# Two-layer transformer kernel, last layer: routing scores spread over scratch memory, scaled rows one batch later, the last network's chunks one at a time inside the last batch's chain

## The chip, the core and the metric

One core of a Trainium2 chip. TensorE (matrix products), VectorE, ScalarE, GpSimd and SyncE work in parallel, each through its own instructions in order; they wait for one another by semaphores. The metric is the device time of one execution, in microseconds.

## The reference

Input x is 8 batches x 256 tokens x 128. Six steps follow, each added to x: self-attention with 16 heads of 8; cross-attention with one head; an expert network; causal attention with one head; cross-attention with 16 heads; and the last network, which matters here:

```python
light_out = feedforward(x, gamma_l, w1_l, b1_l, w2_l, b2_l)
s = jnp.einsum('bnd,d->bn', x, routing_token)
scores = coor_descent(s, N_ITERS, effective_k, EPS)      # 50 steps
selected_scores, selected_indices = jax.lax.top_k(scores, NUM_HEAVY)
routed = jnp.take_along_axis(x, selected_indices[..., None], axis=1)
routed_out = feedforward(routed, gamma_h, w1_h, b1_h, w2_h, b2_h)
heavy_out = jnp.zeros_like(x).at[batch_range, selected_indices].set(routed_out)
```

The 50 steps of `coor_descent` are serial. The 128 best of 256 tokens of a batch go through the heavy network (hidden width 512), all through the light one (64).

## The kernel before, in words

x lies in SBUF as 16 tiles of 128 tokens, two for a batch (NT = 2). The two layers with 16 heads run as one loop each over batches, `for i in steps_of(lo)` with lo = 0 and lo = B = 8. In iteration i and for each head h of 16, TensorE makes the scores of batch i (L1211) for the exponentials of ScalarE (L573), and those of batch i + 1 (L1220) for the row maxima of VectorE (L847). Around them stand, at fixed h, the steps of the neighbouring batches: weighted sums (L1257), transposes of u (L1268) and o (L1274), output projection (L1286), residual (L866), normalisation (L856, L858). In i = 15 no maxima are left. Each engine's order is the order of this code, written by hand; nothing is rearranged.

The last network's work for batch b is laced into the second loop. VectorE takes the statistics (L939, L942) and the product with the routing token (L953); GpSimd makes rstd, scores (`s_tok`, L493) and scales (L503) in `z_norms`; VectorE makes the scaled rows `xr` (L961, `xr_apply`); TensorE transposes them (L1280), ScalarE copies them to `xrT` (L640). GpSimd also splits queries and keys of a coming batch into bf16 parts (L348 to L353, `split`) and adds the light branch's bias (L510).

Every token's rank decides which are taken. VectorE subtracts a token's own score from all 256 of the batch and counts those above (`ranks`, L974, 2 instructions per batch). For this all scores must stand on every partition: TensorE spreads them by two transposes of a broadcast column into PSUM bank `s1_ps[2]` (`spread_scores`, L1298), batches 0 to 4 at h = 2, 5, 8, 11, 14 of i = 15, the rest behind the loop.

Behind the loop TensorE runs hidden chunks `up(q, chunks)` (L1312), five for each pair q of batches, four heavy and one light; ScalarE's GELU follows (L647); `down(q)` (L1521, L1526, L1527) makes the outputs, which ScalarE copies (`branch_copies`, L762, L764). `s_rows` (L1536) brings all scores to 8 rows for the serial steps: 25 + 24 instructions on VectorE (L1088), with an exponential on ScalarE (L756) ahead of each block. Then come the choice (L1109 to L1136), two small transposes (L1507), 16 final combinations (L1147) and four stores.

Exponential and GELU need different tables on ScalarE: a load (ACT_TABLE_LOAD) stands wherever one follows the other. SyncE's queue holds the loads of the split parts into `stack` (L411), in order of batches, and the stores at the end.

## Time and profile before

| | |
|---|---|
| three timed runs, us | 416.61 median, 416.41 to 416.74 |
| the profiled execution, us | 418.83, its span 417.0 |
| busy, share of the span | PE 86%, DVE 78%, ACT 63%, POOL 36% |
| chain that ended last | PE 55%, DVE 26%, ACT 7% |
| row maxima L847 (256) | 162.6 us, 689 ns each |
| attention exponentials L573 (256) | 142.3 us, 597 ns each |
| chain steps L1088 (49) | 24.9 us, 509 ns each |
| hidden chunks L1312 (40 instructions) | 19.3 us, 607 ns each |
| loads of stack, from issue to landing | 2.1 us |

PE is TensorE, DVE VectorE, ACT ScalarE, POOL GpSimd, SP SyncE. Neighbouring instructions of one engine overlap a little in the records, so a sum of durations is longer than the time that they take in a row.

### The profile page before, as it was taken

The page shows a single profiled execution, that of the slowest core. Times are in us where ns is not written, and L with a number is a line of the kernel's source. Part 1 is how long each engine was busy: PE and PEld are TensorE (multiplying, and loading weights), DVE is VectorE, ACT ScalarE, POOL GpSimd, SP SyncE. Part 2 cuts the span into 40 slices and gives each one's busy share as a digit, 9 for nine tenths or more (in the row PEclk, how much of TensorE's full clock was granted, in tenths as well). Part 3 has the DMA queues.
Part 4 walks back from the last instruction along what each step waited for, and adds up shares of the span by engine and source line. Part 5 has one row for each costly group of instructions (what it writes and reads, how often), then busy time and mean ns, then how long its engine had stood idle before and what let it go on. Part 6 is the DMA issues. An engine that isn't in the chain of part 4 may idle for free.

```text
span 417.0 us, 9462 instructions
## 1 busy us (share of the span) xinstructions
PE 358.1 (86%) x3182; PEld 209.9 (50%) x3182; DVE 324.4 (78%) x899; ACT 262.4 (63%) x582; POOL 149.0 (36%) x248
## 2 busy tenths in 40 slices
PE   2788999999999787799968499999989989899791
PEld 1554445444444366379857323444444434456591
DVE  7778699988996338236886497989999997558896
ACT  2245688888888546564553316887877887676630
POOL 8515544665200013001132433356476322451120
PEclk9998899999999969899998956999999999999996
DMA  6432143124430000000000331221311300000003
GB/s 216 114 100 54 53 126 80 42 53 116 118 95 1 2 0 3 0 2 0 2 2 1 89 96 44 59 54 46 78 34 47 78 2 4 0 2 1 2 0 101
DMA packets 35732, 19.98 MB, mean 48 GB/s; under 512 B 4054, under 2 KB 34694, under 8 KB 35686
## 3 DMA queue, kind: packets, MB, share of 16 engines
q1 hardware_dynamic: 34886, 17.81, 16.1%
q10 hardware_dynamic: 608, 1.18, 0.8%
q8 instruction: 26, 0.43, 0.5%
q0 software_dynamic: 192, 0.39, 0.3%
q14 instruction: 20, 0.16, 0.1%
HBM read 5.58 MB, written 1.05 MB: 16 GB/s over the span
## 4 chain that ended last, share of the span: by engine, by line
PE 55%; DVE 26%; ACT 7%; issue 6%; POOL 2%; SPq 2%; DMA 1%; DVEq 0%; ACTq 0%; POOLq 0%
DVE negmax_sb L847 12%; PE pv_ps L1257 11%; PE s_ps L1211 10%; PE prep_ps L1167 4%; PE s_ps L1312 3%; DVE late_sb L1088 3%; PE s_ps L1324 3%; ACT probT_sb L573 2%; PE s_ps L1220 2%; PE prep_ps L1171 2%; PE s_ps L1373 2%; PE prep_ps L1194 2%; PE s_ps L1521 2%; PE out_ps L1356 2%; PE out_ps L1286 2%
## 5 line engine op out<-in xcount | busy, mean ns | idle before, releaser
L847 DVE TENSOR_REDUCE negmax_sb<-s_ps 128x2 bf16<-128x512 f32 x256 | 162.6, 689 | 21.7 <-PE s_ps L1220 21.6
L573 ACT ACTIVATE probT_sb<-s_ps 128x512 f32<-128x512 f32 x256 | 142.3, 597 | 32.0 <-PE s_ps L1211 29.8
L1211 PE MATMUL s_ps<-stack_sb 63*128 63x256 bf16 x512 | 91.4, 279 | 7.3 <-ACT probT_sb L573 3.0
L1220 PE MATMUL s_ps<-stack_sb 62*128 62x256 bf16 x512 | 93.8, 286 | 3.9 <-DMA stack_sb<-parts_sb 3.3
L1257 PE MATMUL pv_ps<-probT_sb,v_aug_sb 128*32 128x256 f32 x1024 | 70.2, 393 | 0.5 <-ACT probT_sb L573 0.5
L1211 PEld LDWEIGHTS s_ps<-stack_sb 63*128 63x128 bf16 x512 | 31.1, 95 | 65.7 <-ACT probT_sb L573 40.2
L449 POOL TENSOR_SCALAR rstd_sb<-mv_sb 128x2 f32<-128x2 f32 x32 | 7.1, 222 | 118.6 <-DVE mv_sb L816 118.6
L595 ACT ACTIVATE qkf_sb<-prep_ps,b_qkv_sb 128x256 f32<-128x256 f32 x56 | 23.9, 471 | 27.4 <-PE prep_ps L1171 20.1
L1257 PEld LDWEIGHTS pv_ps<-probT_sb,v_aug_sb 128*32 128x32 f32 x1024 | 27.1, 110 | 26.5 <-issue 15.1
L1220 PEld LDWEIGHTS s_ps<-stack_sb 62*128 62x128 bf16 x512 | 31.1, 96 | 11.5 <-DVE negmax_sb L847 6.0
L907 DVE SCALAR_TENSOR_TENSOR x_all_sb<-out_ps,den_inv_sb,x_all_sb 128x128 f32<-128x128 f32 x32 | 9.8, 346 | 26.5 <-PE out_ps L1356 26.2
L1088 DVE SCALAR_TENSOR_TENSOR late_sb<-late_sb,level_sb,k_inv_sb 8x256 f32<-8x256 f32 x49 | 24.9, 509 | 5.1 <-ACT late_sb L756 3.4
L824 DVE TENSOR_SCALAR xn_sb<-x_all_sb,mv_sb,rstd_sb 128x128 f32<-128x128 f32 x64 | 22.2, 438 | 5.1 <-POOL rstd_sb L451 4.6
L1167 PE MATMUL prep_ps<-xnT_sb,w_att_sb 128*128 128x256 f32 x64 | 23.4, 450 | 1.9 <-ACT xnT_sb L583 0.9
L451 POOL TENSOR_TENSOR rstd_sb<-rstd_sb,minus_half_sb 128x2 f32<-128x2 f32 x32 | 22.9, 717 | 2.7
L348 POOL CAST parts_sb<-qkf_sb 128x512 bf16<-128x512 f32 x13 | 7.9, 610 | 42.8 <-ACT qkf_sb L595 39.1
L1312 PE MATMUL s_ps<-xrT_sb,d_w_sb 128*128 128x512 f32 x40 | 19.3, 607 | 3.3 <-ACT late_sb L647 3.2
L662 ACT ACTIVATE prob_sb<-s_ps,negbias_sb 128x256 f32<-128x256 f32 (+1 forms) x32 | 14.0, 445 | 7.8 <-DVE negbias_sb L897 7.7
L608 ACT ACTIVATE maxrow_sb<-prep_ps 8x256 bf16<-8x256 bf16 x32 | 11.4, 357 | 9.9 <-PE prep_ps L1205 9.9
L1159 PE MATMUL prep_ps<-ident_sb,xn_sb 128*128 128x128 f32 x30 | 7.2, 328 | 12.0 <-DVE xn_sb L824 10.3
L459 POOL TENSOR_TENSOR x_all_sb<-x_all_sb,b_vo_sb 128x256 f32<-128x256 f32 x16 | 12.1, 763 | 13.4 <-DVE xn_sb L824 13.3
L564 POOL TENSOR_TENSOR ctxT_sb<-ctxT_sb,d_b_sb 128x256 f32<-128x256 f32 x8 | 6.9, 862 | 26.5 <-ACT ctxT_sb L762 26.5
(186 smaller groups left out, 660.8 us busy)
## 6 DMA issues: line engine op xcount, KB each, us to landing
stack_sb<-parts_sb SPq DMA_DIRECT2D x186, 64.0 KB, 2.1
x_all_sb<-x SPq DMA_DIRECT2D x4, 256.0 KB, 3.0
ctxT_sb<-ctxT ACTq DMA_DIRECT2D x2, 512.0 KB, 6.5
f_w_sb<-f_w SPq DMA_DIRECT2D x2, 512.0 KB, 3.8
out<-x_all_sb SPq DMA_DIRECT2D x4, 256.0 KB, 2.4
d_w_sb<-d_w SPq DMA_DIRECT2D x2, 320.0 KB, 4.2
w_att_sb<-w_att SPq DMA_DIRECT2D x2, 256.0 KB, 4.3
stack_sb<-maxrow_sb ACTq DMA_DIRECT2D x32, 4.0 KB
```

Source lines behind the costliest of these rows:

```text
L451: pool.tensor_tensor(rstd[:, u, :], rstd[:, u, :], minus_half[:, 0:NT], ALU.pow).then_inc(rstd_ready, 1)
L573: act.activation(probT[:, c % 8], s2_ps[c % 2][:, :, :], ACT.Exp, scale=DH ** -0.5).then_inc(exp_ready, 1)
L595: act.activation(qkf[:, n % 2, a, :], prep_ps[:, a, :], ACT.Identity, bias=b_qkv[:, n // B, a:a + 1]).then_inc(qk_ready, 2 if n // B == 1 ...
L662: act.activation(prob[:, r % 2, k, 0:w], s1_ps[r % 2][:, k, 0:w], ACT.Exp, bias=negbias[:, r % 2, k:k + 1], scale=D ** -0.5, accum_out=den ...
L824: i = dve.tensor_scalar(xn[:, u, k, :], x_all[:, tiles(n).start + k, :], mv[:, u, k, 0:1], rstd[:, u, k:k + 1], ALU.subtract, ALU.mult)
L847: dve.tensor_reduce(negmax[:, n % 2, :, max_column(max_head(h))], s1_ps[c % 3][:, :, :], axis=AX.X, op=ALU.max, negate=True).then_inc(max_ ...
L1088: dve.scalar_tensor_tensor(out=min_junk[:, :], in0=e_row[:, :], scalar=level[:, a:a + 1], in1=k_inv[:, :], op0=ALU.min, op1=ALU.mult, accu ...
L1167: i = pe.matmul(prep_ps[:, 0, :], w_att[:, l, 0, :], xnT[:, u, :], start=True, stop=True)
L1211: i = pe.matmul(s2_ps[c % 2][:, k, :], stack[rows, s3, 1, h // 2, k * P:(k + 1) * P], stack[rows, s3, 0, h // 2, :], start=True, stop=True)
L1220: i = pe.matmul(s1_ps[c % 3][:, k, :], stack[rows, s3, 0, hp, k * P:(k + 1) * P], stack[rows, s3, 1, hp, :], start=True, stop=True)
L1257: i = pe.matmul(pv_ps[0][32 * j:32 * j + 32, g // 2, :], v_cols[:, k, first:first + 32], probT[:, h % 8, k, :], start=(g % 2 == 0 and k == ...
L1312: pe.matmul(up_bank(c), d_w1[:, f, :], xrT[:, 2 * S * q:2 * S * (q + 1)], start=True, stop=True).then_inc(d_h_psum, 1)
```

## The change

The ranks' scores of batches 0 to 5 go from SBUF to scratch memory in DRAM and from there to all partitions, by SyncE's queue behind the stack loads, into the space of `k_ctx`. Tokens lie there as (p, t) instead of (t, p), so VectorE reads every second element. Batches 6 and 7 are spread by TensorE as before. `xr_apply` moves from h = 12 of iteration b + 10 to h = 2 of b + 11, the transposes to h = 13 of it, ScalarE's copy from h = 0 to h = 13 of b + 11; those of batch 5 go behind the loop. The light bias moves by one batch on GpSimd. Behind the loop the order of the chunks and of the output copies changes. `mask_of_ranks` is written elsewhere but issued at the same place.

```diff
...
 
-RANKED = 5
+SPREAD = 6
 TOP = 80.0
...
         rank_junk = sb("rank_junk", [P, S])
+        others = k_ctx[:, :].rearrange("p (b q) -> p b q", q=S)
         rank = sb("rank", [P, NT, B])
...
         mask_ready, others_psum, rank_ready, rank_psum = sem("mask_ready"), sem("others_psum"), sem("rank_ready"), sem("rank_psum")
+        s_kept, others_in = sem("s_kept"), sem("others_in")
         xr_ready, xrT_psum, xrT_ready, light_bias = sem("xr_ready"), sem("xrT_psum"), sem("xrT_ready"), sem("light_bias")
...
                         load_for_later(i)
+            for b in range(SPREAD):
+                sp.wait_ge(s_tok_ready, b + 1)
+                sp.dma_start(t["s_kept"][b].rearrange("(p k) -> p k", k=NT), s_tok[:, b, :]).then_inc(s_kept, 16)
+                sp.wait_ge(s_kept, 16 * (b + 1))
+                sp.dma_start(others[:, b, :], t["s_kept"][b].partition_broadcast(P)).then_inc(others_in, 16)
             for c in range(4):
...
                 if lo == B:
-                    mask_of_ranks()
                     for n in range(B, 3 * B + AHEAD_C):
...
                         z_norms(n - lo - 5)
-                    if lo == B and n >= lo + 6:
-                        light_bias_(n - lo - 6)
+                    if lo == B and n >= lo + 7:
+                        light_bias_(n - lo - 7)
                     if n not in FIRST:
                         split(pool, n)
+                    if n == B - 1:
+                        mask_of_ranks()
                     if lo == 0 and B // 2 > n - 3 >= 0:
...
                 if b < B - 1:
-                    light_bias_(b - 1)
+                    light_bias_(b - 2)
             xr_last()
-            light_bias_(B - 2)
-            light_bias_(B - 1)
+            for b in range(B - 3, B):
+                light_bias_(b)
             for b in range(B):
...
                             v_copy(i + 3)
-                        if h == 0 and lo == B and has(i - 3, lo):
+                        if h == 13 and lo == B and has(i - 3, lo):
                             xrT_copy(i - 3 - B)
...
 
-            def branch_copies(q):
+            def branch_copies(b):
 
-                for b in (2 * q, 2 * q + 1):
-                    act.wait_ge(d_y_psum, 2 * b + 1)
-                    act.activation(heavy[:, NT * b:NT * b + NT, :], heavy_bank(b), ACT.Copy).then_inc(heavy_copied, 1)
-                    act.wait_ge(d_y_psum, 2 * b + 2)
-                    act.activation(x_all[:, last_tiles(b), :], light_bank(b), ACT.Copy).then_inc(light_done, 1)
+                act.wait_ge(d_y_psum, 2 * b + 1)
+                act.activation(heavy[:, NT * b:NT * b + NT, :], heavy_bank(b), ACT.Copy).then_inc(heavy_copied, 1)
+                act.wait_ge(d_y_psum, 2 * b + 2)
+                act.activation(x_all[:, last_tiles(b), :], light_bank(b), ACT.Copy).then_inc(light_done, 1)
 
...
             xrT_copy(B - 3)
-            hiddens(0, (2, 3))
+            hiddens(0, (2,))
             xrT_copy(B - 2)
-            hiddens(0, (4,))
+            hiddens(0, (3, 4))
             hiddens(1, range(NC))
...
             branch_copies(0)
+            branch_copies(1)
             xrT_copy(B - 1)
             hiddens(2, range(NC))
-            branch_copies(1)
-            shift_exp(1)
-            hiddens(3, range(NC))
             branch_copies(2)
+            shift_exp(1)
             branch_copies(3)
+            hiddens(3, range(NC))
+            for b in range(4, B):
+                branch_copies(b)
 
...
                     dve.wait_ge(mask_ready, 2 * NT + 1)
-                dve.wait_ge(others_psum, b + 1)
+                if b < SPREAD:
+                    dve.wait_ge(others_in, 16 * (b + 1))
+                    above = others[:, b, :].rearrange("p (i t) -> p t i", t=NT)
+                else:
+                    dve.wait_ge(others_psum, b + 1 - SPREAD)
+                    above = s1_ps[2][:, 0, :].rearrange("p (t i) -> p t i", t=NT)
                 for k in range(NT):
...
                         dve.wait_ge(rank_ready, c)
-                    dve.scalar_tensor_tensor(out=rank_junk[:, :], in0=s1_ps[2][:, 0, :], scalar=s_tok[:, b, k:k + 1], in1=rank_mask[:, k, :],
+                    dve.scalar_tensor_tensor(out=rank_junk[:, :].rearrange("p (t i) -> p t i", t=NT), in0=above, scalar=s_tok[:, b, k:k + 1],
+                                             in1=rank_mask[:, k, :].rearrange("p (t i) -> p t i", t=NT),
                                              op0=ALU.subtract, op1=ALU.is_gt, accum_out=rank[:, k, b:b + 1]).then_inc(rank_ready, 1)
...
                                 z_route(i - 2 - B)
-                            if h == 12:
-                                xr_apply(i - 2 - B)
+                        if lo == B and has(i - 3, lo) and h == 2:
+                            xr_apply(i - 3 - B)
                         if i == 2 * B - 1 and h % 3 == 2:
...
             z_norm_stats(B - 2)
+            xr_apply(B - 3)
             z_route(B - 2)
             normalise(2 * B - 1)
-            ranks(RANKED)
+            ranks(SPREAD - 1)
             xr_apply(B - 2)
...
                 pe.wait_ge(s_tok_ready, b + 1)
-                if b == 0:
-                    pe.wait_ge(max_ready, 2 * H * B)
-                if b >= 1:
+                if b > SPREAD:
                     pe.wait_ge(rank_ready, NT * b)
...
                         both_scores(i, h, has(i, lo), has(i + 1, lo))
-                        if i == 2 * B - 1 and h % 3 == 2:
-                            spread_scores(h // 3)
                         if h == 1 and has(i - 1, lo):
...
                             out_project(i - 1)
-                        if h == 15 and lo == B and has(i - 2, lo) and i - 2 < lo + B - 1:
+                        if h == 13 and lo == B and has(i - 3, lo):
                             if prep_free:
                                 pe.wait_ge(*prep_free)
-                            xr_transpose(i - 2 - B)
-                            prep_free = (xrT_ready, i - 2 - B + 1)
+                            xr_transpose(i - 3 - B)
+                            prep_free = (xrT_ready, i - 3 - B + 1)
 
...
             pe.wait_ge(xrT_ready, 2)
-            up(0, (0, 1))
+            pe.wait_ge(max_ready, 2 * H * B)
             weighted_sum(2 * B - 1, 3)
-            spread_scores(RANKED)
+            up(0, (0,))
             u_transpose(2 * B - 1)
+            up(0, (1,))
             o_transpose(2 * B - 1)
-            pe.wait_ge(maxT_ready, 4 * B)
-            up(0, (2, 3))
+            pe.wait_ge(xrT_ready, B - 3)
+            xr_transpose(B - 3)
+            up(0, (2,))
             out_project(2 * B - 1)
...
             xr_transpose(B - 2)
-            up(0, (4,))
-            pe.wait_ge(xrT_ready, 4)
+            up(0, (3, 4))
             pe.wait_ge(exp_ready, 2 * H * B)
-            up(1, (0, 1, 2))
+            up(1, (0,))
             s_rows()
             spread_scores(B - 1)
-            up(1, (3, 4))
+            up(1, (1, 2, 3, 4))
             pe.wait_ge(xrT_ready, B - 1)
...
     dram = {k: nc.dram_tensor(k, a.shape, mybir.dt.from_np(a.dtype), kind="ExternalInput").ap() for k, a in arrays.items()}
+    dram["s_kept"] = nc.dram_tensor("s_kept", (SPREAD, S), fp32).ap()
     dram["out"] = nc.dram_tensor("out", (B, S, D), fp32, kind="ExternalOutput").ap()
```

On TensorE, before, from the last score transposes inside i = 15 to those of batch 6 (s_ps<-stack_sb are scores, L1312 chunks, L1257 the weighted sum):

```order
L1298 MATMUL s_ps<-ident_sb,s_tok_sb 128x128 x2
L1211 MATMUL s_ps<-stack_sb 128x256 x2
L1286 MATMUL out_ps<-w_att_sb,oT_sb 128x128 x2
L1280 MATMUL prep_ps<-ident_sb,xr_sb 128x128 x2
L1312 MATMUL s_ps<-xrT_sb,d_w_sb 128x512 x2
L1257 MATMUL pv_ps<-probT_sb,v_aug_sb 32x256 x8
L1298 MATMUL s_ps<-ident_sb,s_tok_sb 128x128 x2
L1268 MATMUL out_ps<-ident_sb,uT_sb 128x128 x4
L1274 MATMUL out_ps<-ident_sb,o_tok_sb 128x128 x2
L1312 MATMUL s_ps<-xrT_sb,d_w_sb 128x512 x2
L1286 MATMUL out_ps<-w_att_sb,oT_sb 128x128 x2
L1298 MATMUL s_ps<-ident_sb,s_tok_sb 128x128 x2
```

The same place after (L1227 is L1211, L1273 is L1257, L1326 is L1312, L1284, L1290, L1296, L1302, L1312 are L1268, L1274, L1280, L1286, L1298):

```order
L1227 MATMUL s_ps<-stack_sb 128x256 x4
L1302 MATMUL out_ps<-w_att_sb,oT_sb 128x128 x2
L1273 MATMUL pv_ps<-probT_sb,v_aug_sb 32x256 x8
L1326 MATMUL s_ps<-xrT_sb,d_w_sb 128x512
L1284 MATMUL out_ps<-ident_sb,uT_sb 128x128 x4
L1326 MATMUL s_ps<-xrT_sb,d_w_sb 128x512
L1290 MATMUL out_ps<-ident_sb,o_tok_sb 128x128 x2
L1296 MATMUL prep_ps<-ident_sb,xr_sb 128x128 x2
L1326 MATMUL s_ps<-xrT_sb,d_w_sb 128x512
L1302 MATMUL out_ps<-w_att_sb,oT_sb 128x128 x2
L1312 MATMUL s_ps<-ident_sb,s_tok_sb 128x128 x2
L1296 MATMUL prep_ps<-ident_sb,xr_sb 128x128 x2
```

The weighted sum stands ahead of all chunks, and chunks stand singly between the transposes and the projection.

On VectorE, before, one iteration of the second loop from the normalised rows (L824) on:

```order
L824 TENSOR_SCALAR xn_sb<-x_all_sb,mv_sb,rstd_sb 128x128 x2
L847 TENSOR_REDUCE negmax_sb<-s_ps 128x2
L939 BN_STATS z_stats_sb<-x_all_sb 128x6 x2
L942 BN_AGGR z_mv_sb<-z_stats_sb 128x2 x2
L847 TENSOR_REDUCE negmax_sb<-s_ps 128x2
L856 RECIPROCAL den_inv_sb<-out_ps 128x32
L858 TENSOR_TENSOR o_tok_sb<-out_ps,den_inv_sb 128x256
L847 TENSOR_REDUCE negmax_sb<-s_ps 128x2 x3
L953 SCALAR_TENSOR_TENSOR s_junk_sb,s_raw_sb<-x_all_sb,z_mv_sb,route_sb 128x128 x2
L847 TENSOR_REDUCE negmax_sb<-s_ps 128x2 x5
L961 TENSOR_SCALAR xr_sb<-x_all_sb,z_mv_sb,xr_scale_sb 128x128 x2
L847 TENSOR_REDUCE negmax_sb<-s_ps 128x2 x3
```

The same place after:

```order
L833 TENSOR_SCALAR xn_sb<-x_all_sb,mv_sb,rstd_sb 128x128 x2
L970 TENSOR_SCALAR xr_sb<-x_all_sb,z_mv_sb,xr_scale_sb 128x128 x2
L856 TENSOR_REDUCE negmax_sb<-s_ps 128x2
L948 BN_STATS z_stats_sb<-x_all_sb 128x6 x2
L951 BN_AGGR z_mv_sb<-z_stats_sb 128x2 x2
L856 TENSOR_REDUCE negmax_sb<-s_ps 128x2
L865 RECIPROCAL den_inv_sb<-out_ps 128x32
L867 TENSOR_TENSOR o_tok_sb<-out_ps,den_inv_sb 128x256
L856 TENSOR_REDUCE negmax_sb<-s_ps 128x2 x3
L962 SCALAR_TENSOR_TENSOR s_junk_sb,s_raw_sb<-x_all_sb,z_mv_sb,route_sb 128x128 x2
L856 TENSOR_REDUCE negmax_sb<-s_ps 128x2 x8
```

The scaled rows stand right behind the normalised rows, and eight maxima follow the routing product without them.

On ScalarE, before, from the GELUs of q = 2 (L647) to those of q = 3, with output copies (L762, L764) and the second exponential (L756):

```order
L647 ACTIVATE late_sb<-s_ps,d_b_sb 128x512 x5
L762 ACTIVATE ctxT_sb<-s_ps 128x256
L764 ACTIVATE x_all_sb<-prep_ps 128x256
L762 ACTIVATE ctxT_sb<-s_ps 128x256
L764 ACTIVATE x_all_sb<-out_ps 128x256
L756 ACT_TABLE_LOAD
L756 ACTIVATE late_sb<-late_sb 8x256
L647 ACT_TABLE_LOAD
L647 ACTIVATE late_sb<-s_ps,d_b_sb 128x512 x5
```

The same place after:

```order
L655 ACTIVATE late_sb<-s_ps,d_b_sb 128x512 x5
L769 ACTIVATE ctxT_sb<-s_ps 128x256
L771 ACTIVATE x_all_sb<-prep_ps 128x256
L764 ACT_TABLE_LOAD
L764 ACTIVATE late_sb<-late_sb 8x256
L769 ACTIVATE ctxT_sb<-s_ps 128x256
L771 ACTIVATE x_all_sb<-out_ps 128x256
L655 ACT_TABLE_LOAD
L655 ACTIVATE late_sb<-s_ps,d_b_sb 128x512 x5
```

The exponential with its table load stands between the copies of batch 2 and of batch 3.

## Rows read from the trace of the kernel before

**Rows 1.** Stretches: start:end, length, busy us of each engine (instructions), clock, DMA:
```profile
251.00:265.00 14.00, 12.41 (x124) 5.38 (x126) 10.43 (x18) 9.42 (x21) 5.67 (x7) 0.78 0.12 30
265.04:278.56 13.52, 13.29 (x164) 6.66 (x160) 12.28 (x27) 11.40 (x26) 5.72 (x7) 1.00 0.26 65
278.56:293.08 14.52, 13.62 (x162) 6.67 (x158) 14.41 (x37) 11.22 (x25) 8.29 (x15) 1.00 0.21 53
293.08:307.94 14.86, 14.01 (x166) 6.65 (x158) 14.73 (x37) 11.72 (x27) 8.98 (x16) 1.00 0.22 55
...
346.50:358.90 12.40, 11.43 (x119) 5.36 (x117) 7.76 (x33) 10.03 (x20) 3.31 (x9) 1.00 0.01 3
358.90:373.30 14.40, 13.05 (x60) 6.24 (x59) 8.62 (x39) 8.89 (x15) 7.93 (x19) 1.00 0.00 1
373.30:409.30 36.00, 31.32 (x216) 25.05 (x214) 30.69 (x118) 19.69 (x34) 8.41 (x11) 1.00 0.00 1
```

**Rows 2.** VectorE's scaled rows: all 14 of L961, then three pairs in the timeline:
```profile
L961 DVE TENSOR_SCALAR xr_sb<-x_all_sb,z_mv_sb,xr_scale_sb x14: 337/342/1318, 288.9 to 365.2; 128x128 f32<-128x128 f32 x14
...
288.95 1.43 DVE L961 TENSOR_SCALAR xr_sb<-x_all_sb,z_mv_sb,xr_scale_sb 128x128 f32<-128x128 f32 x2
...
303.48 1.81 DVE L961 TENSOR_SCALAR xr_sb<-x_all_sb,z_mv_sb,xr_scale_sb 128x128 f32<-128x128 f32 x2
...
331.96 0.59 DVE L961 TENSOR_SCALAR xr_sb<-x_all_sb,z_mv_sb,xr_scale_sb 128x128 f32<-128x128 f32 x2
```

**Rows 3.** GpSimd's timeline: start us, us, engine, line, operation, idle before:
```profile
295.75 0.73 POOL L459 TENSOR_TENSOR x_all_sb<-x_all_sb,b_vo_sb 128x256 f32<-128x256 f32 x1 [0.78 <-DVE xn_sb L824]
...
304.05 1.16 POOL L350 TENSOR_TENSOR rest_sb<-qkf_sb,parts_sb 128x512 f32<-128x512 f32 x1
...
376.05 0.76 POOL L564 TENSOR_TENSOR ctxT_sb<-ctxT_sb,d_b_sb 128x256 f32<-128x256 f32 x1 [1.24 <-ACT ctxT_sb L762]
```

**Rows 4.** TensorE: the score transposes (L1298), then its timeline in the last part:
```profile
L1298 PE MATMUL s_ps<-ident_sb,s_tok_sb x16: 272/273/323, 347.9 to 371.3; 128*128 128x128 f32 x16
...
360.76 1.07 PE L1257 MATMUL pv_ps<-probT_sb,v_aug_sb 128*32 128x256 f32 x16
...
366.43 0.61 PE L1286 MATMUL out_ps<-w_att_sb,oT_sb 128*128 128x128 f32 x4
...
371.37 1.88 PE L1312 MATMUL s_ps<-xrT_sb,d_w_sb 128*128 128x512 f32 x4
...
407.47 0.39 PE L1527 MATMUL out_ps<-d_w_sb,late_sb 128*128 128x128 f32 x2
```

**Rows 5.** ScalarE's timeline in the last part:
```profile
357.60 1.28 ACT L573 ACTIVATE probT_sb<-s_ps 128x512 f32<-128x512 f32 x2 [0.55 <-PE s_ps L1211]
...
374.00 1.28 ACT L756 ACT_TABLE_LOAD   x1
...
387.27 0.38 ACT L764 ACTIVATE x_all_sb<-prep_ps 128x256 f32<-128x256 f32 x1 [0.51 <-PE prep_ps L1527]
...
391.64 0.41 ACT L756 ACTIVATE late_sb<-late_sb 8x256 f32<-8x256 f32 x1
...
393.37 1.26 ACT L647 ACTIVATE late_sb<-s_ps,d_b_sb 128x512 f32<-128x512 f32 x2
```

**Rows 6.** SyncE's stack loads, their landing, the scores (GpSimd), VectorE's chain:
```profile
299.93 31.33 SPq L411 DMA_DIRECT2D stack_sb<-parts_sb  x26
...
stack_sb<-parts_sb SPq DMA_DIRECT2D x186, 64.0 KB, 2.1
...
352.56 0.19 POOL L493 TENSOR_TENSOR s_tok_sb<-s_raw_sb,z_rstd_sb 128x2 f32<-128x2 f32 x1 [1.34 <-DVE s_junk_sb L953]
...
369.67 0.19 POOL L493 TENSOR_TENSOR s_tok_sb<-s_raw_sb,z_rstd_sb 128x2 f32<-128x2 f32 x1
...
376.26 0.82 DVE L1088 SCALAR_TENSOR_TENSOR late_sb<-late_sb,level_sb,k_inv_sb 8x256 f32<-8x256 f32 x1
...
390.30 0.34 DVE L1076 TENSOR_SCALAR late_sb<-late_sb,shift_sb 8x256 f32<-8x256 f32 x1
```

4 lines of the change are left out of this document (2 added, 2 removed).

## The prediction

> **What bounds the kernel now.** I read the table of stretches first [rows 1]. The last attention layer works one batch after another; a stretch is one batch, from one step of VectorE to the same step of the next batch. In the stretch before the router's work begins (265.04 to 278.56, 13.52 us) TensorE is busy 13.29 us and VectorE 12.28: TensorE sets the pace. In the next two (14.52 and 14.86; the third, to 322.80, reads like the second) VectorE is busy 14.41 and 14.73: VectorE sets the pace. Two of about 12.4 us follow, with VectorE as full. In the last one (346.50 to 358.90) VectorE has slack (7.76 busy); TensorE is busy 11.43 of 12.40 and ScalarE 10.03.
>
> Next VectorE's scaled rows, L961 [rows 2]. A pair takes 0.59 us at 331.96 and 1.81 at 303.48; the median of one is 342 ns, the longest 1318. The reader is to see beside the 1.81 what GpSimd does [rows 3]: its L350 runs from 304.05 to 305.21, and the pair ends at 305.29. So VectorE loses this time to GpSimd, not to arithmetic.
>
> Last the timelines of TensorE and ScalarE to the end [rows 4, 5]. The end hangs on a serial chain of 49 steps on VectorE in two blocks, with an exponential on ScalarE ahead of each. The first exponential waits for ScalarE's table load at 374.00, right behind the tenth GELU; the second begins at 391.64.
>
> **Term 1, scaled rows one batch later.** L961 of batch b moves from the 13th reduction of one iteration to the third of the next. Before, five pairs lie in full stretches and take VectorE 1.35, 1.73, 1.73, 0.52 and 0.52 us (the 1.43, 1.81 and 0.59 of [rows 2] less the 0.08 that the next reduction overlaps), together 5.85. After, four lie there, as the fifth falls in the slack one: at 0.52 each 2.1. The new place has a neighbour too: right behind the normalised rows (L824) GpSimd adds a bias, 0.73 us from 295.75 [rows 3]. In two of the four iterations this add can hold up the second scaled row by up to 0.73, so 2.1 to 3.6, and 2.3 to 3.8 saved on VectorE. TensorE keeps part of it: its own pace is the 13.52 of the undisturbed stretch, and 13.7 with the two transposes now at h = 13 (0.22). The three long stretches (44.2) fall to 13.5 + 13.7 + 13.7 = 40.9 at best, and to 13.5 + 14.4 + 14.4 = 42.3 if each add is met (14.86 - 1.73 + 0.52 + 0.73 = 14.4). That is 1.9 to 3.3; I take 2.3, near the lower end, since two engines within 0.3 us of each other seldom interlock without loss. The later copy of the transposed rows (ScalarE) and the light branch's bias (GpSimd) fall on engines busy 11.7 and 9.0 of 14.86 [rows 1]: nothing.
>
> **Term 2, scores over scratch memory.** In the last batch five pairs of transposes (L1298, 273 ns each, two of them some 0.36 in the queue) leave TensorE, 1.8 us [rows 4]. The pair of the scaled rows stays in the batch. TensorE's 11.43 becomes 9.6, with ScalarE's 10.03 beside it, which now idles 12.40 - 10.03 = 2.4. If ScalarE's pace decides nearly alone, 0.3 is saved; if all five count, 1.8. I take 1.0. In it is that ScalarE's copy, now at h = 13, waits for a weighted sum and the transposes ahead of it, some 0.3.
>
> The waits added: SyncE's queue has issued its last stack load at 331.26 [rows 6]. Then, per batch, a store, a wait for it, and a load to 128 partitions. No row shows such a store; a stack load lands in 2.1 us [rows 6] and the kernel's other loads in 2.1 to 4.5, so a round trip is 4.2 to 9. Batch 0 lands by 340.3 at the latest and is wanted at about 347.5; the next follow every 2 to 4.5. Batch 5, whose scores are made at 352.56 [rows 6], lands between 357 and 362 and is wanted behind the last normalisation, at about 362. Behind the waiting comparison stand, on VectorE, normalisation and residual of the last batches. Only the top of the bound touches them: nothing. Behind SyncE's waits stand only the output stores, 50 us later.
>
> A comparison (L974) takes 0.48 with one input in PSUM; now both are in SBUF, one with a stride. The nearest row is the chain's step (L1088), the same operation with both inputs in SBUF: 0.51 on the mean of 49, 0.82 at 376.26, behind a GpSimd add that began at 376.05 [rows 3, 6]. So 0 to 0.35 more for each of 12. Ten lie in the slack of the last batch; two behind the last normalisation, where up to 0.7 reach the chain. I keep 0.2 of that in term 3. The Trainium skill ("SBUF — State Buffer", section "Who interferes with whom") has a rule against this edit: a VectorE instruction with two SBUF inputs contends with a GpSimd instruction that reads SBUF, one with a single such input does not. The 0.82 agrees in kind. By the rule alone the two late comparisons would meet GpSimd's scaling and give the whole 0.7: a sum smaller by 0.5.
>
> **Term 3, the last batch's chain and the two exponentials.** Before, two chunks of the hidden layer (L1312) run on TensorE ahead of the last weighted sum, which starts at 360.76 though the last exponential ended at 358.88 [rows 4, 5]; two more run ahead of the output projection (366.43), and the score row stands behind four. After, the weighted sum comes first and single chunks fill the waits. From 358.90 to the end of the tenth chunk (371.37 + 1.88 = 373.25) TensorE is busy 13.05 of 14.40 [rows 1, 4]. Its 1.35 of idling can go, and one pair of transposes goes (0.2): 1.6. It need not all come: GpSimd makes the last scores 3.4 us behind the projection's start (366.43 to 369.86 [rows 4, 6]), and TensorE asks for them 0.45 + 2 x 0.22 + 3 x 0.94 = 3.7 behind it (projection, two pairs, three chunks at half of 1.88), so that wait is nil or some tenths. Bounds 0.8 and 2.0 (the chunks' own gaps go as well); I take 1.6 less the 0.2 of the comparisons = 1.4.
>
> The second exponential: its shift is ready at 390.30 + 0.34 = 390.64 [rows 6], but ScalarE copies the fourth output first and then loads the table, 1.28; it starts at 391.64 [rows 5]. In the new order it stands behind the third output, whose copy ends at 387.65 (387.27 + 0.38). Table and shift both move with the chain; the load would then end 390.64 - 387.65 - 1.28 = 1.7 before the shift is ready. The 1.0 us of waiting is gone, covered by those 1.7. What is late next: exponential 0.4, two copies 0.7, GELU's table 1.3, so the next GELU starts 2.4 behind an exponential that comes at 390.64, 0.3 earlier than the 393.37 of now on the same clock. TensorE's last product (407.47 + 0.39 = 407.86 [rows 4]) moves by 1.4 + 0.3 = 1.7, to 406.2, and the chain's weights, ready at 409.3, by 2.4, to 406.9. It stays hidden by 0.7. Term 3: 1.4 + 1.0 = 2.4, bounds 1.8 and 3.0.
>
> **Sum.** 2.3 + 1.0 + 2.4 = 5.7 us. The profiled execution took 418.83 with a span of 417.0 and becomes 413.1. The three timed runs have a median of 416.61, 2.2 below the profiled one: 410.9. With the lower bounds (1.9 + 0.3 + 1.8 = 4.0) 412.6, with the upper (3.3 + 1.8 + 3.0 = 8.1) 408.5.
>
> **Rivals.**
> A. TensorE or ScalarE holds the three long stretches where they are. For it: TensorE is busy 14.01 of 14.86 in one of them [rows 1]. Against: it did the same work in 13.29 the batch before. Terms 2 and 3 are left, 3.4: 413.2. Chance 0.13.
> B. The last batch's chain moves, the 49 steps hardly do: the first exponential still comes when the tenth GELU does, and TensorE loses the 1.6 in waits for single GELUs. For it: the waits are short and many. Term 3 is then the 1.0 of the second exponential: 416.6 - 4.3 = 412.3. Chance 0.13.
> C. Slower: TensorE's clock falls between 350 and 371, where it now has less to do. The stretch 251 to 265 shows a granted clock of 0.78 [rows 1], a mix of 2.4 and 1.2 GHz, and at 1.2 its work lasts twice as long. Each us of its work there at the lower level costs one us; from 6 on the kernel is slower, and with 10 it takes 421. Against: 31.32 busy of 36.00, a share of 0.87, kept 1.00 [rows 1], and 9.6 of 11.4 is 0.84. Chance 0.04.
> D. The change does not do what it says: the round trips come so late that VectorE waits as long as TensorE saves. The first would have to take some 22 us (347.5 - 331.3 + 5.7), against a bound of 9. No change, 416.6. Chance 0.04.
> E. More: the upper bounds, and fewer meetings of chain steps with GpSimd's adds (0.35 each): 407.5. Chance 0.05.
>
> **How the numbers follow.** The forecast, 410.9 with its own range 408.5 to 412.6, has 0.61. About 0.2% (0.8 us) is what a measurement of this kernel can tell from no change. Faster 0.61 + 0.13 + 0.13 + 0.05 = 0.92, same 0.04, slower 0.04. The range 407.7 to 413.8 leaves out C, D, half of E and the tails of A and B.
>
> **What will show it.** Right: scaled rows in pairs of 0.6 to 1.3 us and the three long stretches at 13.5 to 14.4; no score transposes within the last batch, and that batch at 11.4; ScalarE's table load 1.4 us closer to the last attention exponential than the 15.1 of now (374.00 - 358.88); the second exponential within 0.1 of its shift. Wrong: a wait of VectorE for a load, long stretches still near 14.8, a granted clock under 1.00 after 350, or a last transpose of the weights that waits for TensorE's products and not for VectorE.

## The result and the profile after

The changed kernel takes 422.49 us (median of 4 runs, 420.99 to 423.67), the one before 416.68 beside it (416.41 to 417.33). The ratio is 1.0142, with a 95% interval of 1.0111 to 1.0172: slower, where 410.9 was forecast. The profiled execution took 422.39 with a span of 420.6.

I looked first where the changed kernel is late. The timeline of SyncE's queue from the last stack load on (start us, us) shows the round trips (the first, the second and the last are printed; ... marks what is left out here and below); L423 is a store to scratch memory, L425 a load from it:

```profile
330.34 0.59 SPq L423 DMA_DIRECT2D s_kept<-s_tok_sb  x1
334.31 0.33 SPq L425 DMA_DIRECT2D k_ctx_sb<-s_kept  x1
334.68 0.55 SPq L423 DMA_DIRECT2D s_kept<-s_tok_sb  x1
341.50 0.32 SPq L425 DMA_DIRECT2D k_ctx_sb<-s_kept  x1
...
358.29 0.43 SPq L423 DMA_DIRECT2D s_kept<-s_tok_sb  x1
363.71 0.32 SPq L425 DMA_DIRECT2D k_ctx_sb<-s_kept  x1
```

The chain of waits in the same stretch (328 to 372) gives what a trip is made of, and the view of transfers the medians from issue to landing (KB each, us):

```profile
334.68 6.81 DMA s_kept<-s_tok_sb
...
341.86 5.81 DMA s_kept<-s_tok_sb
...
358.29 5.41 DMA s_kept<-s_tok_sb
363.71 4.31 DMA k_ctx_sb<-s_kept
```
```profile
k_ctx_sb<-s_kept SPq DMA_DIRECT2D x6, 128.0 KB, 4.3
...
s_kept<-s_tok_sb SPq DMA_DIRECT2D x6, 1.0 KB, 5.3
```

The store of 1 KB takes longer than the load of 128 KB. A trip's load waits for its store to land, and the next trip's store goes out right behind that load, without waiting for it. So the trips follow one another at the time of one store each: the stores are issued 4.3, 7.2, 6.2, 4.7 and 5.5 us apart. The stores hold 71.5% of the chain from 328 to 372. [Rows 6] had the queue free at 331.26, and there was no row for a store. VectorE's timeline in the last batch shows who waits (the bracket is the idle time before the instruction, and what ended it):

```profile
356.70 0.49 DVE L988 SCALAR_TENSOR_TENSOR rank_junk_sb<-k_ctx_sb,s_tok_sb,rank_mask_sb 128x256 f32<-128x256 f32 x1 [2.63 <-DMA k_ctx_sb<-s_kept]
...
362.42 0.49 DVE L988 SCALAR_TENSOR_TENSOR rank_junk_sb<-k_ctx_sb,s_tok_sb,rank_mask_sb 128x256 f32<-128x256 f32 x1 [4.70 <-DMA k_ctx_sb<-s_kept]
...
368.05 0.77 DVE L988 SCALAR_TENSOR_TENSOR rank_junk_sb<-k_ctx_sb,s_tok_sb,rank_mask_sb 128x256 f32<-128x256 f32 x1 [1.63 <-DMA k_ctx_sb<-s_kept]
```

That is 9.0 us in three waits, for batches 3, 4 and 5. Behind the comparisons of batch 3 VectorE has only those of batch 4, which wait themselves; behind batch 4's stand a residual, statistics, scaled rows and the last normalisation, behind batch 5's scaled rows and the last residual. So TensorE's last chain starts late and waits for VectorE's L875, L867 and L970 (1.67, 1.05 and 1.36 us). The stretches, in the columns of [rows 1], answer to its third and fourth row; the last is ten us of the last batch:

```profile
278.05:291.81 13.76, 13.19 (x160) 6.47 (x156) 13.24 (x35) 11.22 (x25) 7.96 (x15) 1.00 0.22 56
291.81:307.12 15.31, 13.80 (x162) 6.69 (x158) 14.19 (x36) 11.65 (x26) 8.62 (x16) 1.00 0.22 55
...
360.00:370.00 10.00, 5.79 (x36) 2.96 (x37) 5.77 (x24) 4.60 (x7) 3.33 (x9) 1.00 0.12 26
```

The second stretch is the surprise: VectorE is busy 14.19, 0.54 less than before, and yet the stretch is 15.31 and not 14.86. The third (307.12 to 322.43) is 15.31 too, so the three long stretches take 44.4 us, where 44.2 stood before and 40.9 to 42.3 were forecast. VectorE waits in the second, for the scores of h = 14 and 15, behind the place (h = 12) where the scaled rows used to stand:

```profile
304.36 0.70 DVE L856 TENSOR_REDUCE negmax_sb<-s_ps 128x2 bf16<-128x512 f32 x1 [0.51 <-PE s_ps L1236]
305.55 0.70 DVE L856 TENSOR_REDUCE negmax_sb<-s_ps 128x2 bf16<-128x512 f32 x1 [0.49 <-PE s_ps L1236]
```

The scaled rows themselves are shorter, as forecast (longest 786 ns, against 1318 in [rows 2]):

```profile
L970 DVE TENSOR_SCALAR xr_sb<-x_all_sb,z_mv_sb,xr_scale_sb x14: 332/342/786, 294.3 to 369.5; 128x128 f32<-128x128 f32 x14
```

At the end the second exponential is 0.04 us behind its shift (1.0 in [rows 5, 6]) and the transposes of the weights wait for VectorE, 1.51 us as before. VectorE's timeline, then ScalarE's, then TensorE's:

```profile
394.29 0.34 DVE L1092 TENSOR_SCALAR late_sb<-late_sb,shift_sb 8x256 f32<-8x256 f32 x1
```
```profile
391.72 1.28 ACT L764 ACT_TABLE_LOAD   x1
394.67 0.41 ACT L764 ACTIVATE late_sb<-late_sb 8x256 f32<-8x256 f32 x1 [1.66 <-DVE late_sb L1092]
```
```profile
412.92 0.28 PE L1519 MATMUL s_ps<-ident_sb,late_sb 8*128 8x8 f32 x2 [1.51 <-DVE late_sb L1152]
```

**A measure that doesn't shift.** The part up to the router's first statistics is nearly the same work in all these kernels, yet it ended between 277.0 and 281.6 us in their traces. So I compare traces from there: "the five stretches" below are the time from the first statistics of the scores (281.59 before, 281.08 after) to those of the sixth batch (349.41 and 349.79), that is 67.82 us before and 68.71 after. "From the first statistics to the end" is the time from there to the end of the span: 135.41 before (417.0 - 281.59) and 139.52 after (420.6 - 281.08). Medians are of up to 12 runs each; on the chips of the experiments the kernel before took 416.7 to 417.1.

### The profile page after: what moved, and what is told of

Its sections match the earlier page's. It is cut to its first block, busy times and chain, and to the rows that moved or that the text cites. A ratio compares the mean times of both kernels' runs of the same rounds, so it can differ in the third digit from the quotient of the medians.

```text
span 420.6 us, 9443 instructions
## 1 busy us (share of the span) xinstructions
PE 357.6 (85%) x3170; PEld 208.9 (50%) x3170; DVE 323.5 (77%) x899; ACT 263.1 (63%) x582; POOL 148.9 (35%) x248
## 3 DMA queue, kind: packets, MB, share of 16 engines
HBM read 6.37 MB, written 1.05 MB: 18 GB/s over the span
## 4 chain that ended last, share of the span: by engine, by line
PE 50%; DVE 20%; DMA 9%; ACT 7%; issue 5%; POOL 4%; SPq 4%; DVEq 0%; ACTq 0%; POOLq 0%
PE pv_ps L1273 11%; PE s_ps L1227 10%; DMA s_kept<-s_tok_sb 7%; DVE late_sb L1104 6%; DVE negmax_sb L856 5%; PE prep_ps L1183 4%; SPq L413 3%; PE s_ps L1338 3%; PE prep_ps L1187 2%; PE s_ps L1236 2%; ACT probT_sb L581 2%; PE s_ps L1387 2%; PE prep_ps L1210 2%; PE out_ps L1370 2%; PE prep_ps L1175 2%
## 5 line engine op out<-in xcount | busy, mean ns | idle before, releaser
L1227 PE MATMUL s_ps<-stack_sb 63*128 63x256 bf16 x512 | 92.0, 278 | 9.5 <-ACT probT_sb L581 4.5
L1273 PE MATMUL pv_ps<-probT_sb,v_aug_sb 128*32 128x256 f32 x1024 | 70.3, 393 | 1.1 <-ACT probT_sb L581 1.1
L1227 PEld LDWEIGHTS s_ps<-stack_sb 63*128 63x128 bf16 x512 | 31.2, 95 | 67.1 <-ACT probT_sb L581 41.9
L1273 PEld LDWEIGHTS pv_ps<-probT_sb,v_aug_sb 128*32 128x32 f32 x1024 | 27.1, 110 | 26.5 <-issue 15.2
L1326 PE MATMUL s_ps<-xrT_sb,d_w_sb 128*128 128x512 f32 x40 | 19.8, 610 | 2.7 <-ACT late_sb L655 2.7
L655 ACT ACTIVATE late_sb<-s_ps,d_b_sb 128x512 f32<-128x512 f32 x20 | 13.5, 686 | 6.3 <-PE s_ps L1326 6.3
```

What stands on the lines that cost most here:

```text
L1227: i = pe.matmul(s2_ps[c % 2][:, k, :], stack[rows, s3, 1, h // 2, k * P:(k + 1) * P], stack[rows, s3, 0, h // 2, :], start=True, stop=True)
L1273: i = pe.matmul(pv_ps[0][32 * j:32 * j + 32, g // 2, :], v_cols[:, k, first:first + 32], probT[:, h % 8, k, :], start=(g % 2 == 0 and k == ...
L1326: pe.matmul(up_bank(c), d_w1[:, f, :], xrT[:, 2 * S * q:2 * S * (q + 1)], start=True, stop=True).then_inc(d_h_psum, 1)
```

## The experiments

In the expectations T1 is the theory that the serial round trips hold VectorE in the last batch; T2, that TensorE's transposes and ScalarE's copy at h = 13 cost the loop its time.

**One part undone at a time.** The scratch trips undone:

```diff
-            for b in range(SPREAD):
-                sp.wait_ge(s_tok_ready, b + 1)
-                sp.dma_start(t["s_kept"][b]..., s_tok[:, b, :]).then_inc(s_kept, 16)
...
+                        if i == 2 * B - 1 and h % 3 == 2:
+                            spread_scores(h // 3)
```

> The changed kernel with its scores spread by TensorE again (batch 5 behind the last weighted sum), the later scaled rows and the new tail kept. Theory T1: the scratch round trips, one behind the other at 5.6 us each, hold VectorE in the last batch (its three waits for loads, 9.0 us in sum). Theory T2: the copy and the transposes of the scaled rows at h = 13 hold up the scores and cost the loop 3.3 us. By the trace of the change both act: the loop ends 3.3 later (349.79 against 346.50), which leaves 2.5 of the 5.8 us, and the tail's gain of about 2.4 on top of it, 4.9 for the trips. So T1 and T2 together: 422.5 - 4.9 = 417.6, no wait of VectorE for a load, the loop still at 349.8. T1 alone: 414 or less, loop back at 346.5. T2 alone: 422.5, since the waits for loads would only stand in for others.

Measured: 417.93 us, ratio to before 1.0018 (0.9986 to 1.0049). As expected of both theories together: not one wait for a load, and the loop still long, 69.96 for the five stretches. That is more than 68.71, since the score transposes stand in the last of them again.

The later scaled rows undone:

```diff
-                        if lo == B and has(i - 3, lo) and h == 2:
-                            xr_apply(i - 3 - B)
+                            if h == 12:
+                                xr_apply(i - 2 - B)
```

(with the transposes back at h = 15, the copy at h = 0, and GpSimd's light bias back at its old place)

> The changed kernel with the scaled rows, their transposes and their copy back at their old places; scratch trips and new tail kept. T2: the loop gets its 3.3 us back, 419.2; the waits of VectorE for PE's scores between 260 and 350 fall from 5.7 to about 2.2 us and the collisions of the scaled rows with GpSimd (1.4 to 1.8 a pair) return. T1 alone: the round trips run by the clock of SyncE's queue from the last stack load on, so the time stays at 422.5 if the loop does not get shorter. If the stack load moves with the loop, the trips move with it and the 3.3 come whole.

Measured: 423.05, ratio 1.0129 (1.0086 to 1.0172): nothing gained. But the five stretches took 66.33, 2.4 less than 68.71. SyncE's queue in this trace, first store and last load:

```profile
326.96 0.59 SPq L423 DMA_DIRECT2D s_kept<-s_tok_sb  x1
...
361.73 0.32 SPq L425 DMA_DIRECT2D k_ctx_sb<-s_kept  x1
```

VectorE's waits for loads rose from 9.0 to 13.0 us instead. The last load is issued 84.7 us behind the first statistics (361.73 - 277.02), in the change 82.6 us (363.71 - 281.08): the trips began 0.7 us later and took 1.4 longer, and had swallowed the gain. The end follows the last load and not the loop: it comes 57.0 us behind that load's issue here (418.7 - 361.73) and 56.9 in the change (420.6 - 363.71).

Both undone, the tail alone on the kernel before:

> The kernel before with the new tail alone: single chunks in the last batch's chain, and the second exponential ahead of the fourth output's copy. The forecast's third term: 416.7 - 2.4 = 414.3, the second exponential within 0.1 us of its shift. Rival T3 (the single chunks only trade one wait for another, the 49 steps hardly move): 415.7, the second exponential's 1.0 alone. If the tail is itself at fault: above 416.7.

Measured: 414.99, ratio 0.9952 (0.992 to 0.9983): the tail is worth 2.1 us, where 2.4 was forecast. The trace has less: from the statistics of the sixth batch to the first of the 49 steps 25.48 us against 26.33, and from there to the last step 28.83 against 29.37, 1.4 in sum. The second exponential comes 0.03 behind the end of its shift, but the block of steps behind it took 0.5 longer than before.

**The round trips overlapped.** The same stores and loads, in another order:

```diff
-            for b in range(SPREAD):
+            for group in ((0, 1, 2, 3), (4,), (5,)):
+                for b in group:
...
                 sp.wait_ge(s_kept, 16 * (b + 1))
+                for b in group:
```

> The changed kernel with the round trips overlapped: the stores of batches 0 to 3 are issued one behind the other, one wait, then their four loads; batches 4 and 5 follow one at a time. T1: batches 0 to 3 land by about 342, batch 4 by 352, batch 5 by 362, instead of 338 to 357, 362 and 368; VectorE's waits for loads shrink from 9.0 to 1 us or less and the time falls by 4 to 5 us, to about 418. T2 alone: 422.5. If a store's 4 to 7 us are a cost of the bytes or descriptors (128 of 8 bytes) and not of the wait for completion, four stores in a row take 16 to 27 us, batch 0 comes at 350 to 357, and the time stays at 422 or above.

Each load has a semaphore of its own here. Measured: 416.75, ratio 0.9978 (0.9951 to 1.0006). By medians 5.7 us come back, a little more than expected; by the traces, from the first statistics to the end, 4.1 (139.52 to 135.39). SyncE's queue in its trace:

```profile
326.56 2.01 SPq L424 DMA_DIRECT2D s_kept<-s_tok_sb  x4
333.02 1.74 SPq L427 DMA_DIRECT2D k_ctx_sb<-s_kept  x4
339.29 0.32 SPq L424 DMA_DIRECT2D s_kept<-s_tok_sb  x1
342.19 0.32 SPq L427 DMA_DIRECT2D k_ctx_sb<-s_kept  x1
349.83 0.32 SPq L424 DMA_DIRECT2D s_kept<-s_tok_sb  x1
352.98 0.32 SPq L427 DMA_DIRECT2D k_ctx_sb<-s_kept  x1
```

Four stores are done in 6.5 us, and the two single ones, with no load ahead of them, in 2.9 and 3.15. VectorE waits for no load.

**Is the store slow, or what stands ahead of it?** The opposite edit, more waiting:

```diff
                 sp.dma_start(others[:, b, :], t["s_kept"][b].partition_broadcast(P)).then_inc(others_in, 16)
+                sp.wait_ge(others_in, 16 * (b + 1))
```

> The changed kernel with SyncE waiting for each load to land before it issues the next store, so that no store follows a load in the queue. It tells what made the stores slow (4.0 to 6.8 us, 5.3 in the middle). If a load still on its way ahead of it in the queue did: every store takes 2.9 to 4 us and every load 3 to 4.3, a trip is 7 us instead of 5.6 to 6.8, six take 42 us, the last lands near 372 and the time is 424 to 427. If the store itself is slow by its layout: stores stay at 5.3, a trip is 9.6, the last lands at 388 and the time is over 435.

Measured: 428.84 (2 runs), ratio 1.0305. The landing times (min, median, max) of the stores and of the loads:

```profile
DMA to landing us min/median/max: 3.0/3.7/4.2
...
DMA to landing us min/median/max: 3.4/4.0/4.3
```

So a store falls from 5.3 to 3.7 when no load is on its way ahead of it, and a load from 4.3 to 4.0. The trip, 7.1 to 8.2 us now, was a little longer than I expected, and the time is 1.8 above the top of what I expected. The last load is issued at 371.29, and VectorE waits 16.6 us. By the medians the load ahead in the queue costs a store 1.6 us; the other 3.7 us of each store pass before its completion is seen, with or without a load ahead.

**The stores on a queue of their own.**

```diff
                 pool.tensor_tensor(s_tok[:, b, :], ...).then_inc(s_tok_ready, 1)
+                if b < SPREAD:
+                    pool.wait_ge(s_tok_ready, b + 1)
+                    pool.dma_start(t["s_kept"][b]..., s_tok[:, b, :]).then_inc(s_kept[b], 16)
```

> The changed kernel with each store issued by GpSimd on its own queue right behind the row of scores it makes; SyncE only waits for it and issues the load. Place of rows and tail as in the change. T1: the stores of batches 0 to 3 are long done when SyncE's last stack load has gone out at about 330, so four loads follow at once and land by about 337; batch 5 lands by 354 + 3 + 4.3 = 361. No wait of VectorE for a load, 416.7 as with overlapped stores. A store that shares no queue with a load takes 3 us or less, against 4.0 to 6.8 in the change, if the load ahead of it in the same queue is what made it slow; it takes 5 still if the layout (128 pieces of 8 bytes) does. What can go wrong: GpSimd's issue of a DMA delays the adds behind it, some 1 us a batch, which ScalarE and VectorE do not wait for.

Measured: 417.93, ratio 1.0019 (0.9989 to 1.0049). No wait for a load, and stores of 3.4 in the median. But it is 1.2 above the overlapped trips, and VectorE's timeline has what I had called harmless: GpSimd's issue (0.67 us, and 0.3 to wait for its own product) makes the reciprocal deviation late.

```profile
292.43 0.60 DVE L834 TENSOR_SCALAR xn_sb<-x_all_sb,mv_sb,rstd_sb 128x128 f32<-128x128 f32 x2 [0.67 <-POOL rstd_sb L456]
```

That stretch is 15.34, against 14.73 with the trips overlapped.

**Where the loop's time goes.** All that follow have the trips overlapped (but for one) and the new tail. First the old places of rows, transposes and copy:

> Overlapped round trips with the scaled rows, transposes and copy at their old places; new tail kept. With the trips one behind the other, undoing the shift gave nothing (423.05), though it shortened the stretch from the first statistics of the scores to the last batch's by 2.4 us (66.33 against 68.71). T1 with T2 (the trips run by the clock of their queue and had swallowed the 2.4): now the 2.4 come through, 416.75 - 2.4 = 414.3, about 0.7 below the new tail alone (414.99). If the shift at h = 13 costs nothing: 416.7 as with overlapped trips alone.

Measured: 413.41, ratio 0.9924 (0.9891 to 0.9956), the fastest kernel of this study, 1.6 below the tail alone (by the traces, from the first statistics to the end, 1.0: 133.01 against 134.01). The stretches with all three at the new places (68.70 in sum, trace of the overlapped trips), and at the old (66.33), with the light bias back too:

```profile
292.04:307.35 15.31, 13.79 (x158) 6.67 (x154) 14.19 (x36) 11.66 (x26) 8.30 (x15) 1.00 0.24 59
...
sum 68.70, PE 62.82 PEld 29.46 DVE 64.47 ACT 53.77 POOL 30.95; mean PE 12.56 PEld 5.89 DVE 12.89 ACT 10.75 POOL 6.19
```
```profile
291.81:306.67 14.86, 13.68 (x157) 6.59 (x158) 14.73 (x36) 11.40 (x25) 8.98 (x17) 1.00 0.19 48
...
sum 66.33, PE 61.74 PEld 29.33 DVE 65.83 ACT 52.77 POOL 31.57; mean PE 12.35 PEld 5.87 DVE 13.17 ACT 10.55 POOL 6.31
```

VectorE is busy 1.4 us more at the old places and the sum is 2.4 us less. Then T2's own test, transposes at h = 15 and copy at h = 0, rows left at h = 2:

```diff
-                        if h == 13 and lo == B and has(i - 3, lo):
+                        if h == 15 and lo == B and has(i - 3, lo):
...
                             xr_transpose(i - 3 - B)
```

> Overlapped round trips; scaled rows one iteration later as in the change, but their two transposes behind the output projection at h = 15 and ScalarE's copy at h = 0, as before the change. T2 says that the loss lies in the place h = 13 of transposes and copy and the gain in the place of the scaled rows: VectorE's waits for scores from the first statistics of the scores to the last batch's fall from 5.0 us to about 2, the pairs of scaled rows stay at 0.6 to 1.04, and the stretch takes 68.7 - 3.3 = 65.4; the time is 416.75 - 3.3 = 413.4, a little below the run with the old places. If the loss comes with VectorE's place itself: 416.7.

Measured: 415.83, ratio 0.9972 (0.9944 to 0.9999), the five stretches 68.38. That is 0.3 of the 2.4 in the stretches, where T2 asked for all of it and more, and T2 falls. The same with TensorE's scores for the trips:

> As the run before this one, with TensorE's spread scores in place of the round trips: the new tail, scaled rows one iteration later, transposes at h = 15, copy at h = 0. T2: 417.93 - 3.3 = 414.6, or less, as it should not be above the new tail alone (414.99) but for noise. It prices the scratch memory at its best against TensorE's transposes: by term 2 of the forecast it is 1.0 to 1.5 us slower than with overlapped trips.

Measured: 418.44, ratio 1.0032 (1.0005 to 1.0059), far above what T2 asked for and 2.6 above the trips (by the traces, from the first statistics to the end, 0.9: 135.77 against 134.84). The other half was tried next: VectorE's rows back at h = 12 and the light bias with them, transposes and copy left at h = 13.

> Overlapped round trips and new tail, as in the last runs. VectorE's scaled rows at their old place (h = 12 of their own iteration), but TensorE's transposes and ScalarE's copy of them at h = 13 of the next iteration, as in the change. Moving transposes and copy back alone gave only 0.3 us of the 2.4 in the stretches, so theory T2 (their place costs the loop) is in doubt. Theory T4: the loss lies in VectorE's place. At h = 12 the rows, collision with GpSimd and all, stand where TensorE's scores come late anyway (h = 11 to 15 hold the transposes of the outputs, a weighted sum and both projections), so they were free; at h = 2 they make a row of non-reductions of 1.6 us that TensorE, three heads ahead at most, waits out. T4: stretches of 66.3 to 66.7 in sum from the first statistics of the scores to the last batch's (66.33 with all three at the old places, 68.70 with all three at the new), VectorE's waits for scores there near 1.2, rows at 1.4 to 1.8 a pair again, 413.5. T2: 68 or more, waits of 4 us, 415.5.

Measured: 414.82, ratio 0.9962 (0.9936 to 0.9987); the five stretches 66.63, waits for scores 1.2, as T4 said. The time is 1.3 above its 413.5, a little more than the 1.0 us of its interval.

```profile
293.27:308.13 14.86, 13.69 (x157) 6.58 (x158) 14.73 (x36) 11.55 (x25) 8.98 (x17) 1.00 0.22 53
...
sum 66.63, PE 61.95 PEld 29.12 DVE 66.06 ACT 53.07 POOL 31.58; mean PE 12.39 PEld 5.82 DVE 13.21 ACT 10.61 POOL 6.32
```

So 2.1 of the 2.4 us go with VectorE's rows and GpSimd's light bias, which moved together, and not with TensorE's transposes and ScalarE's copy. Two other places of the rows:

> Overlapped trips and new tail, VectorE's scaled rows at h = 14 of their own iteration: two heads later than before, past GpSimd's L350, which ends 1.7 us after they began at h = 12; transposes at h = 1 and copy at h = 2 of the next iteration. It takes the collision away and leaves the rows among TensorE's dense heads. T4: pairs of 0.6 us in all stretches, yet little gained, since VectorE then waits for scores what it waited for GpSimd: 66.33 less 0 to 1 in sum, 412.5 to 413.5. If the collision was a real loss and only the place h = 2 was wrong: the three pairs of 1.44, 1.81 and 1.81 shrink to 0.6 each, 3.3 us less, 410.

Measured: 416.79, ratio 1.0015 (0.9986 to 1.0043), the five stretches 68.20. It misses both numbers: the pairs still met GpSimd (2.35, 1.49, 1.49 us), and the next transposes of maxima waited 1.9 us for the copy at h = 2. Rows, transposes and copy all moved, so it decides nothing between the theories.

> Overlapped trips and new tail; VectorE's scaled rows at h = 5 of the next iteration, between two stretches of GpSimd's work (it is idle there from 293.8 to 296.6 in the trace with overlapped trips) and past the cluster of h = 2 to 4; transposes at h = 15, copy at h = 0 of the iteration after. Pairs of 0.59 us everywhere. If the collision was a real loss and h = 2 only a bad place: 66.33 less 1 to 3 in sum, 411 to 412.5. If the rows' time was free at h = 12 (T4), anything placed elsewhere costs up to its full 0.5 us a stretch: 66.5 to 69, 413.5 to 416.

Measured: 415.59, ratio 0.9957 (0.9926 to 0.9988), the five stretches 66.98, all pairs at 0.59 or 0.60. No collision is left and nothing is gained over h = 12. Against the run with rows at h = 2 and transposes at h = 15 (68.38) only VectorE's place differs, and the light bias is at its new place in both: 1.4 of the 2.1 us are VectorE's place alone. The other 0.7, against 66.33, was not divided between the place h = 5 and the light bias. Last the plain question, whether that time at h = 12 sets the pace at all:

```diff
-                for k in range(NT):
+                for k in range(1):
                     i = dve.tensor_scalar(xr[:, b % 2, k, :], ...
```

> Overlapped trips, new tail, rows at their old places, but of each batch's two scaled rows at h = 12 the second is left out (its tile holds zeros), all else the same: VectorE has 0.25 to 1.2 us less to do there. The stretches were 14.52, 14.86, 13.63, 12.39 and 10.93 us (66.33). If VectorE set the pace there, as the forecast's first term has it, the first three fall to 13.7 or so, to 64 in sum. If the rows' time was free at h = 12 (theory T4), they stay within 0.3 each, 66 in sum, and VectorE waits longer for scores at h = 13 to 15 (1.2 us in sum now, 3 or more then).

Measured: 414.38, ratio 0.9943 (0.9909 to 0.9977). The first three stretches and the sum, and VectorE's waits for scores from 262 to 345 (1.2 with both rows):

```profile
277.56:292.09 14.53, 13.66 (x157) 6.58 (x158) 13.46 (x35) 11.40 (x25) 8.30 (x16) 1.00 0.19 49
292.09:306.62 14.53, 13.66 (x157) 6.58 (x158) 13.70 (x35) 11.40 (x25) 8.97 (x17) 1.00 0.20 49
306.62:320.25 13.63, 13.16 (x153) 6.36 (x152) 12.60 (x29) 11.14 (x25) 7.66 (x14) 1.00 0.24 60
...
sum 66.18, PE 61.54 PEld 29.31 DVE 62.59 ACT 52.52 POOL 31.56; mean PE 12.31 PEld 5.86 DVE 12.52 ACT 10.50 POOL 6.31
```
```profile
DVE negmax_sb L858 <- PE s_ps L1238: 4.2, 11, 0.7
```

VectorE loses 3.2 us of work (65.83 to 62.59) and the sum loses 0.15. It waits for scores instead, 3.1 us within the five stretches where it had no such wait; in the second stretch that is 0.69, ahead of the reduction at 302.97, the first behind the residual that ends an iteration. The stretches do not all stand still: the second falls by 0.33 (14.86 to 14.53), the fourth grows by 0.43 (12.39 to 12.82). In sum, and from the first statistics to the end (133.14 against 133.01), the second scaled row, collision and all, was free at h = 12.

## Why the prediction was wrong

**The account.** By medians: tail -2.1 (414.99 against 417.11), overlapped trips in place of TensorE's scores -1.6 (413.41), rows, transposes and copy one iteration later +3.3 (416.75), trips in series +5.7 (422.5). The sum is +5.3, and the change measured +5.8. The traces close better. From the first statistics to the end they give 135.41 before, 134.01 with the tail, 133.01 with overlapped trips, 135.39 with the later rows and 139.52 with the trips in series: -1.4, -1.0, +2.4 and +4.1, in sum +4.1. The loss is 4.1 us in the part that was changed; the other 1.7 of the medians' 5.8 is not explained; ahead of the first statistics the traces themselves differ by up to 4.6 us (277.0 to 281.6). The first two are the gains that were forecast; the other two were forecast as a gain of 2.3 and as nothing.

**Term 2, the step that failed first: the waits added, "the next follow every 2 to 4.5" and "Only the top of the bound touches them: nothing".** The order of the queue was read rightly: each store goes out right behind the load of the trip before, so the trips follow at the time of one store each. What was wrong is that time. It was bounded by the landing of loads, 2.1 to 4.5 us, as there was no row for a store (and even of the loads the longest was left out, 6.5 us for 512 KB). The six stores took 3.95 to 6.81 us, 5.3 in the median, and with the issues the trips came 4.3 to 7.2 us apart. The last scores landed at 368.02, where 357 to 362 was written. Even inside my bounds "nothing" did not follow: with 4.5 us a trip batch 5 lands at 340.3 + 5 x 4.5 = 362.8, just later than it is wanted. Batches 3 and 4 I never compared with the moment when they are wanted, and in the trace VectorE waited for both (2.63 and 4.70 us). Rival D named this very wait, with a chance of 0.04, and then asked the wrong thing of it: a first trip of 22 us. The first store was inside the bound, at 3.95 us; four of the five behind it were not, and their excess added up. The overlapped trips show that the wait for each store's completion was the fault and not scratch memory, and the trips apart, that more waiting makes it worse by 6.3 us.

The other half of term 2, 1.0 us for TensorE's five pairs of transposes, was right: 1.6 by medians and 1.0 by the traces. The fifth stretch is 10.93 us against 12.41, and 0.5 of it is lost again between the sixth statistics and the first of the 49 steps (25.96 us against 25.48). The comparisons from SBUF cost what a bound of zero says, 485 ns in the median against 484 before, and one of twelve took 767, beside GpSimd's add of 367.81. The rule quoted from the Trainium skill ("SBUF — State Buffer", "Who interferes with whom") agrees with the trace for that one; the 0.2 us kept for it was enough. As the prediction gives it, the rule lacks an exception that the section makes: in the modes in which it uses both of its ports, open to TENSOR_SCALAR, VectorE contends with GpSimd with a single input in SBUF too. The scaled rows are such an instruction, and [rows 2] have one at 1318 ns beside GpSimd, where 342 is the median; which mode they ran in no run here shows.

**Term 1, the other step that failed: "VectorE loses this time to GpSimd", so the long stretches fall to 13.5 and 14.4.** The first half is right and the second doesn't follow. The pairs shrank as priced (1.04, 1.04, 0.59 and 0.59 in the full stretches, 2.9 in sum less the overlap of 0.08 each, where 2.1 to 3.6 stood), but the three long stretches grew from 44.2 to 44.4 us. A busy share of 14.73 in 14.86 says that VectorE is never idle. It does not say that a shorter VectorE ends the stretch earlier, for TensorE was busy 14.01 of the same 14.86, and it hands VectorE its scores through three PSUM banks. One row of each pair left out moved the sum of the five stretches by 0.15. Rival A had this mechanism (TensorE holds the stretches, 0.13), and it too would have lost only the gain. What no case had is that the new place costs: by the traces +2.4 at h = 2, of which 0.3 are the transposes and the copy, at least 1.4 VectorE's place, and up to 0.7 the light bias, which was not moved by itself; rows in h = 12 are free. That the reason is TensorE's dense end of the iteration (h = 11 to 15) against its short reach ahead at h = 2 fits the waits, 0.51 and 0.49 at 304 to 306, and the run with a row left out. It is argued and not shown: the reach itself was not varied.

**Term 3** had its mechanisms right and its size too large: forecast 2.4, 2.1 by medians (the interval is 0.7 to 3.3) and 1.4 by the trace, the chain's start 0.85 earlier where 1.4 stood, the second exponential's 1.0 us gone but half of it lost again in the second block of steps. The output's end stays with VectorE, as said. Rival C (the clock) is out: the granted clock is 1.00, the level of 2.4 GHz, in every stretch above, even from 360 to 370 with TensorE busy 5.79 of 10.

**The signs.** Of the four signs named for a wrong forecast two were seen: a wait of VectorE for a load, first at 356.70, and long stretches not below 14.8 (two of three, at 15.31). The clock did not fall in the stretches above, and the last transposes of the weights waited for VectorE.
